# Another order of the score, weighting and fill matmuls within TensorE's attention period

## The reference

```python
q = _ln(latents, sa_ln_g, sa_ln_b)
x = latents + _mha(q, q, sa_in_w, sa_in_b, sa_out_w, sa_out_b)
qc = _ln(x, ca_q_ln_g, ca_q_ln_b)
kv = _ln(tokens, ca_kv_ln_g, ca_kv_ln_b)
x = x + _mha(qc, kv, ca_in_w, ca_in_b, ca_out_w, ca_out_b)
# in _mha:
scores = jnp.einsum('bhqd,bhkd->bhqk', q, k) / jnp.sqrt(jnp.float32(dh))
attn = jax.nn.softmax(scores, axis=-1)
out = jnp.einsum('bhqk,bhkd->bhqd', attn, v)
```

## Time and profile before

| | |
|---|---|
| median of three runs | 1970.85 us |
| profiled execution / its span | 1970.29 us / 1968.5 us |
| TensorE matmuls busy | 1473.1 us, 75% of the span |
| VectorE busy | 1237.6 us, 63% |
| ScalarE busy | 880.4 us, 45% |
| self-attention, first fill taken to last weighting | from 170 to 893 us |
| its scores begin | 211 us |
| cross-attention, scores to last weighting | from 1088 to 1247 us |
| a take (VectorE), mean, self- / cross-attention | 1.22 / 0.80 us |

### The profile page before, as it was taken

How to read it: one execution, slowest core, us unless ns; L and a number is a source line. 1 busy time by engine, 2 the same in 40 slices (tenths; PEclk the granted TensorE clock), 3 DMA queues, 4 the chain that set the end, 5 groups by cost and what they waited for, 6 DMA issues and landing times. The chain is left out here.

```text
span 1968.5 us, 28844 instructions
## 1 busy us (share of the span) xinstructions
PE 1473.1 (75%) x9920; PEld 740.2 (38%) x9921; DVE 1237.6 (63%) x1664; ACT 880.4 (45%) x1710; POOL 281.2 (14%) x211
## 2 busy tenths in 40 slices
PE   5883888888888888883652877367049999999970
PEld 3440111111111111111431322056038888888860
DVE  4545888898988898921662322088765555555535
ACT  2220587887887787781111544223613222222210
POOL 1000000000000000001310000042713343343320
PEclk8995699999999999996786555577559999999985
DMA  3446011131121111006637253497511122122219
GB/s 103 165 176 151 1 28 28 34 71 28 28 50 28 28 45 33 1 1 144 189 111 103 25 71 59 98 309 235 178 29 54 54 62 59 55 63 56 57 59 320
DMA packets 147398, 166.63 MB, mean 85 GB/s; under 512 B 26747, under 2 KB 115712, under 8 KB 147312
## 3 DMA queue, kind: packets, MB, share of 16 engines
q1 hardware_dynamic: 135600, 140.85, 27.9%
q0 software_dynamic: 7488, 20.46, 3.4%
q10 hardware_dynamic: 4224, 4.19, 0.6%
HBM read 106.83 MB, written 58.36 MB: 84 GB/s over the span
## 5 line engine op out<-in xcount | busy, mean ns | idle before, releaser
L919 DVE TENSOR_REDUCE sa_half_maxs<-sa_psm 128x2 f32<-128x1024 f32 x512 | 603.5, 1221 | 88.8 <-PE sa_psm L814 88.7
L901 ACT ACTIVATE sa_p<-sa_pss 128x512 f32<-128x512 f32 x1024 | 532.7, 603 | 187.0 <-PE sa_pss L850 185.3
L850 PE MATMUL sa_pss<-sa_q,sa_k 49*128 49x512 f16 x1024 | 294.4, 389 | 68.2 <-ACT sa_p L901 65.7
L814 PE MATMUL sa_psm<-sa_k,sa_q 48*128 48x512 f16 x1024 | 255.6, 400 | 38.6 <-DMA sa_ident<-in_ident 20.1
L863 PE MATMUL sa_pso<-sa_p,sa_v 128*32 128x512 f32 x2048 | 275.4, 610 | 0.4 <-ACT sa_p L901 0.2
L1468 ACT ACTIVATE moe_h<-moe_psh,moe_b 128x256 f32<-128x256 f32 x312 | 122.3, 475 | 318.8 <-PE moe_psh L1405 182.2
L850 PEld LDWEIGHTS sa_pss<-sa_q,sa_k 49*128 49x128 f16 x1024 | 72.9, 94 | 438.1 <-ACT sa_p L901 404.8
L1403 PE MATMUL moe_psh<-moe_hh,w_high 128*128 128x256 f16 x624 | 171.2, 274 | 0.0
L1404 PE MATMUL moe_psh<-moe_hl,w_high 128*128 128x256 f16 x624 | 171.1, 274 | 0.0
L1405 PE MATMUL moe_psh<-moe_hh,w_low 128*128 128x256 f16 x624 | 171.1, 274 | 0.0
L1419 PE MATMUL moe_pse<-w_high,moe_h1h 128*128 x624 | 170.1, 273 | 0.3 <-DVE moe_h1l L1494 0.3
(11 more groups left out here) (207 smaller groups left out, 1834.7 us busy)
## 6 DMA issues: line engine op xcount, KB each, us to landing
dram_sa_v<-qkv_v_sb SPq DMA_DIRECT2D x8, 1024.0 KB, 5.4
dram_sa_qk_parts<-qkv_part SPq DMA_DIRECT2D x16, 512.0 KB, 6.8
sa_v<-dram_sa_v SPq DMA_DIRECT2D x16, 512.0 KB
last_w_stage<-in_w SPq DMA_DIRECT2D x8, 1024.0 KB, 7.0
route_stage<-in_w SPq DMA_DIRECT2D x16, 512.0 KB, 4.5
sa_q<-dram_sa_qk_parts SPq DMA_DIRECT2D x96, 64.0 KB
sa_k<-dram_sa_qk_parts SPq DMA_DIRECT2D x96, 64.0 KB
ca_q<-dram_ca_q_parts SPq DMA_DIRECT2D x24, 256.0 KB
```

The lines of the kernel that those rows point to most:

```text
L814: mm = pe.matmul(ps_m[z][:, r, :], q_st[u][rows, j0 + j, qt * P:(qt + 1) * P], k_st[u][rows, j0 + j, half * HALF:(half + 1) * HALF], start ...
L850: pe.matmul(ps_s[S % SBANKS][:], k_st[u][rows, j0 + j, kt * kp:(kt + 1) * kp], q_st[u][rows, j0 + j, half * HALF:(half + 1) * HALF], start ...
L901: act.activation(probs[n % PSLOTS][h][:], ps_s[S % SBANKS][:], ACT.Exp, scale=float(DH) ** -0.5).then_inc(exps, 1)
L919: dv.tensor_reduce(half_maxs[G % 2][:, half, :, c], ps_m[z][:], AX_X, ALU.max).then_inc(taken, 1)
```

## The change

The program of TensorE's period is written in another order; what is computed, the other engines' programs and the buffers stay. The new order is: fill A (and turn), score 0, weighting, score 1, fill B, scores 2 and 3. The order holds for both attentions.

```diff
                 for n in range(groups * per_group):
-                    for h in range(HG // 2):
-                        score(n * HG + h)
                     advance(2 * n + lead)
+                    score(n * HG)
                     if n >= LAG:
                         weigh(n - LAG)
-                    for h in range(HG // 2, HG):
-                        score(n * HG + h)
+                    score(n * HG + 1)
                     advance(2 * n + 1 + lead)
+                    score(n * HG + 2)
+                    score(n * HG + 3)
                 for n in range(groups * per_group - LAG, groups * per_group):
                     weigh(n)
```

## The result

The changed kernel took 1951.05 us, the median of 20 runs, against 1969.28 us for the kernel before (20 runs). The forecast was 1949.9. The ratio of the mean times is 0.9925 with a 95% interval from 0.9908 to 0.9942, so 0.75% less; it leaves out the four slowest runs of the changed kernel (1974.6 to 1978.7 us), which count as slow ones. The profiled execution took 1949.63 us with a span of 1947.8, which is 20.7 under the span before. What they are is the subject of the last experiments.

What follows compares the result with a forecast made beforehand. A loop of waits, scores waiting for exponentials with fill A's second matmul inside, was taken to set the period. Self-attention -25.5 and cross-attention +4.5 on 1970.29 gave 1949.3 us profiled, 1949.9 for the runs; range 1941 to 1962.

Steps and rivals of the forecast that it cites:

- The loop: Self-attention: fill A's second matmul leaves the loop, period 2.38 instead of 2.61 us; 234 x 0.226 = -52.9 us.
- The copy: Self-attention: ScalarE's copy out comes late and holds up the weighting, 0.70 us 31 times, +21.7 us.
- The turn: Self-attention, every 16th period: TensorE waits for VectorE's join, score 0 comes 1.28 us later; 0.52 x 15 = +8.0 us.
- The self-attention: Sum of the self-attention's terms: -26.0 us, taken as -25.5, bounds -30 and -17.
- The cross-attention: Cross-attention at half clock: periods of 4.21 and 4.52 against 4.02 and 4.35 us; +4.5 us taken, bounds 0 and +10.
- The cheap end: Cross-attention: score 2 goes when its own rows are free, period 4.21 us; behind all eight short matmuls it would be 4.43.
- (a): More given back: copies, turns, cross-attention dear, loop 2.42 as fill A waits for VectorE; 1957 to 1965 us, chance 0.12.
- (c): Self-attention loop does not shorten: fill A's slot is hidden anyway or the takes bind; 2004 us, chance 0.05.
- (d): More gain: cross-attention's loss all absorbed, rows in time, clock rising a little sooner; 1941 us, chance 0.08.
- (b): Self-attention: longer stops at turns and copies let TensorE's clock fall, making the kernel slower; chance 0.05.
- the case of 17 such periods: Self-attention: 17 periods at half clock, 3.65 instead of 2.38 us, about one group, eat the 21 us gain.
- the case of four groups: Self-attention: four groups at half clock, 64 periods, cost +81 us and give 2030 us.

Runs made afterwards that it cites:

- f5: Kernel before with fill A alone moved ahead of score 0; four runs of 1925.7, 1931.2, 1947.2 and 1950.4 us.
- f7: Changed kernel with VectorE's self-attention take reading 512 of the 1024 elements; 1930.8 us.
- e3: Changed kernel with ScalarE's copy behind the exponential of score 0 instead of score 2; 1925.3 us profiled, the other four 1943.8 to 1947.5.
- e2: Kernel before with the new order in the cross-attention alone; 1971.7 us in ten runs against 1971.0, ratio 1.0008.
- f8: The kernel of e3 unchanged, run again for a second profile, of the longer kind; 1951.4 us.
- g1: The kernel of e3 plus two unread matmuls in each missing fill's place in the self-attention's last 18 periods; 1928.6 us, ratio 0.9785.
- e4: Changed kernel with the turn moved from behind fill A to behind the weighting; 1948.4 us profiled, 1953.7 median of four, ratio 0.9929.

## Why the prediction was right, and where it was not

**The loop.** Right, by its own steps: exponential 0.42, score 0 at 1.08, weighting 0.31 later, score 1 another 1.00 later; 2.39 instead of 2.38. Fill A waits for the take and is at 0.67 (0.68 forecast). f5 shows that the slot is the cause and f7 that VectorE is not the bound.

**The copy.** 0.66 instead of 0.70, since the weighting follows the copy's end by 0.06 and not 0.10. e3 shows the cause. It took 20 us of the 53.

**The turn.** 3.68, 1.29 over the ordinary period (1.28 forecast); the forecast's product 0.52 x 15 is 7.8 and not 8.0, which changes nothing. Missed was 0.08 two periods behind each turn (2.47), 1.2 us in all. There score 0 is the first of its group:

```profile
252.96 0.39 PE L850 MATMUL sa_pss<-sa_q,sa_k 49*128 49x512 f16 x1
...
254.12 0.37 PE L850 MATMUL sa_pss<-sa_q,sa_k 49*128 49x512 f16 x1
```

It comes 1.16 after score 1 instead of 1.08. That it has two waits, for the exponential and for the row, and score 0 is now on the loop, fits: with short takes it stays, and where score 1 closes the loop (f5) most of these periods are 2.39. It was not tried by itself.

**The self-attention** came out at -25.2 against -25.5. So close a sum has some luck in it. Both periods that had waited for a late row (3.56 and 2.95) are gone, -1.3 where -0.7 was taken, against the +1.2 behind the turns. The clock rose 6.6 us sooner (221.7 instead of 228.3 us), where 3 had been allowed for, while the first score starts 1.3 later.

**The cross-attention.** Periods 4.16 and 4.62 against 4.21 and 4.52, a total of +4.6 against +4.5. The cheap end was the right one: the strict order would have given 4.43. The Trainium skill's rule ("TensorE: Matmul & The Clock Gate", Part 3), that matmuls start strictly in program order, is not what this trace shows between the two halves of the rows. That the total fits is partly luck: the 28 periods outside the three stops lost 6.1 together and the stops got 1.4 shorter, where the forecast let only 22 periods count, +5.0, and gave 1.7 to the stops and 0.6 to the last store. And e2 leaves open how much of the loss arrives at the end.

**The rivals.** (a) is refuted in its mechanism. (c) did not happen, and of (d) only its small terms did: the rows came in time and the clock rose sooner, but the cross-attention's loss was not absorbed. (b) did happen in seven of 20 executions, if these are what f8 shows; no profile of a long execution of this kernel was taken, but their times (23 us above the short ones) and mean clocks (0.830 to 0.835) fit. By its own sign, "or if the clock falls", the prediction was wrong in those. The place was one that I had not named: not within the groups, where a turn stops TensorE for 1.00 and no profile shows a fall, but at the last turn, with a stop of 1.33 and no fills behind it. My price for a period at half clock, 3.65, was near (3.69), and the case of 17 such periods that eat the gain is what came; the case of four groups was too large, and 0.05 was too small a chance. That the profiled execution had a whole clock is luck as well.

Why the ratio says 0.75% where the profiles say 1.05% has two parts. Three long executions are in it; the thirteen short ones alone are 0.93% under the kernel before. The rest is that the profiled execution before, 1970.29, was 1.9 above the mean of its 20 runs. None of the 47 runs of the kernel before here was above 1974.73, where a long one would be near 1991.

## What to carry to other kernels

Find the cycle of waits that sets the period and ask of each matmul between the releasing wait and its end whether it must stand there: one matmul slot moved out of it was worth 40 us net in the self-attention (f5), and 25 as the change had it, in executions that kept the clock. In an in-order queue, list every operation that has a date with another engine, and the slack that each had by accident: the copy had next to none before (it ended 0.10 ahead of the weighting) and cost 0.66 each time after. Look apart at the last periods, where the overlapped work is gone: there the clock fell in some executions and stayed down, and a single profile of a lucky execution did not show it. Compare the mean granted clock of all executions before trusting one profile.

## What was not expected of the hardware

TensorE's clock fell from 2.4 to 1.2 GHz at a stop of 1.33 us followed by lighter periods, in some executions of a program and not in others (f8 and e3), and did not rise in 67 us of weightings and scores at TensorE 93% busy; with two more matmuls in each fill's place it was back after one period of 3.57 (g1). It also fell 31 us after the last turn, with no stop longer than 0.59 in between (e4). Short matmuls of one half of the array's rows started ahead of earlier ones of the other half: four of a fill's eight from 1109.11 on, within 0.18 us, while score 1 held the other half, and the other four only from 1109.54.
